# The mixing of values turned over in both attention layers: probabilities stationary, values moving, tokens on the output's partitions

## The reference, cut to what matters

```python
# x: (16, 256, 128); 16 heads of 8 channels
x = x + attn_a(layernorm(x))     # attention inside blocks of 64 positions
x = x + ffn(layernorm(x))        # 8 experts, top 2 of them per token
x = x + attn_b(layernorm(x))     # the 16 rows attend across each other at each position, with a bias,
                                 # then an output projection
x = x + ffn(layernorm(x))
# attn: softmax(q k^T * scale) @ v for each head
```

## Time and profile before

| | |
|---|---|
| median of three runs | 976.49 us |
| the profiled execution | 975.18 us |
| its span, first to last instruction | 973.4 us |
| mean granted TensorE clock | 0.878 |
| busy: TensorE matmul, weight load | 708.4 us, 583.4 us |
| busy: VectorE, ScalarE, GpSimd | 523.4, 473.5, 396.2 us |

### The profile page before, as it was taken

How to read it: one execution, slowest core, us unless ns; L and a number is a source line. 1 busy time by engine, 2 the same in 40 slices (tenths; PEclk the granted TensorE clock), 3 DMA queues, 4 the chain that set the end, 5 groups by cost and what they waited for, 6 DMA issues and landing times. The chain is left out here.

```text
span 973.4 us, 26881 instructions
## 1 busy us (share of the span) xinstructions
PE 708.4 (73%) x8764; PEld 583.4 (60%) x8765; DVE 523.4 (54%) x1810; ACT 473.5 (49%) x876; POOL 396.2 (41%) x458
## 2 busy tenths in 40 slices
PE   1688877831699999998077898761109999999940
PEld 1356555521588888887035676661108888888830
DVE  3367888863356555554253565642305555555524
ACT  0689877630355555553058897520005555555510
POOL 1223777786033333333231154588732333333320
PEclk9989999975799999999558999985559999999985
DMA  7001222212111111111330000001211111111107
GB/s 204 8 12 45 68 83 87 76 56 67 32 47 47 49 46 47 47 47 36 99 118 24 26 3 10 31 29 39 69 39 41 49 44 49 47 47 49 45 20 259
DMA packets 54045, 54.51 MB, mean 56 GB/s; under 512 B 8272, under 2 KB 43472, under 8 KB 53968
## 3 DMA queue, kind: packets, MB, share of 16 engines
q1 hardware_dynamic: 42608, 32.19, 12.1%
q0 software_dynamic: 8704, 18.11, 5.8%
q10 hardware_dynamic: 2656, 3.15, 0.9%
HBM read 29.51 MB, written 23.90 MB: 55 GB/s over the span
## 5 line engine op out<-in xcount | busy, mean ns | idle before, releaser
L1581 POOL DMA_INDIRECT expert_out<-moe_a_out,moe_a_place x72 | 69.0, 958 | 153.0 <-DVE moe_a_out L1716 153.0
L1581 POOL DMA_INDIRECT expert_out<-moe_b_out,moe_b_place x72 | 69.0, 958 | 152.7 <-DVE moe_b_out L1716 152.7
L1613 PE MATMUL wide<-wgu,moe_a_hi 128*128 x288 | 96.7, 417 | 0.5 <-issue 0.5
L1613 PE MATMUL wide<-wgu,moe_b_hi 128*128 x288 | 96.7, 417 | 0.4 <-issue 0.4
L1629 PE MATMUL wide<-wd,moe_a_hidT 128*128 x576 | 76.4, 276 | 1.1 <-DVE moe_a_out L1716 0.7
L1629 PE MATMUL wide<-wd,moe_b_hidT 128*128 x576 | 76.4, 276 | 1.0 <-DVE moe_b_out L1716 0.7
L1669 ACT ACTIVATE moe_a_glow<-wide 128x512 f32<-128x512 f32 x72 | 43.0, 598 | 69.9 <-PE wide L1613 69.8
L1669 ACT ACTIVATE moe_b_glow<-wide 128x512 f32<-128x512 f32 x72 | 43.0, 598 | 69.6 <-PE wide L1613 69.5
L441 POOL DMA_INDIRECT routed<-la_norm_x,la_place x64 | 63.6, 994 | 23.0 <-issue 19.3
L1629 PEld LDWEIGHTS wide<-wd,moe_a_hidT 128*128 128x128 f32 x576 | 70.0, 192 | 1.7 <-issue 1.7
L1629 PEld LDWEIGHTS wide<-wd,moe_b_hidT 128*128 128x128 f32 x576 | 70.0, 192 | 1.6 <-issue 1.6
(11 more groups left out here) (257 smaller groups left out, 1693.4 us busy)
## 6 DMA issues: line engine op xcount, KB each, us to landing
moe_a_rows<-routed SPq DMA_DIRECT2D x72, 66.0 KB, 1.9
moe_b_rows<-routed SPq DMA_DIRECT2D x72, 66.0 KB, 1.9
lb_outs<-expert_out SPq DMA_DIRECT2D x8, 512.0 KB
la_stage<-in_wg SPq DMA_DIRECT2D x8, 256.0 KB, 2.6
la_stage<-in_wu SPq DMA_DIRECT2D x8, 256.0 KB, 2.8
wd<-in_wd SPq DMA_DIRECT2D x8, 256.0 KB, 3.7
kept<-stream SPq DMA_DIRECT2D x8, 256.0 KB, 3.6
stream<-kept SPq DMA_DIRECT2D x8, 256.0 KB
```

The costliest lines, as they stand in the source:

```text
L1581: pool.indirect_dma_start(d.expert[:, :], bass.IndirectOffsetOnAxis(ap=place[s % 4][:, 0:1], axis=0), out[u][:, :], None).then_inc(stored[ ...
L1613: last = nc.tensor.matmul(ps[u][:, :], x[u][:, :], w(j, part), start=i == 0, stop=i == 2)
```

## The change

`mixing` swaps its operands in both layers: the transposed probabilities are loaded as weights and `stand` moves past them, so that tokens come out on the partitions and head channels on the free axis. In the first layer that is 64 stationary columns and 18 moving ones in two column strips of 64; in the second 32 stationary and 36 moving ones in four strips of 32. The number of products stays 32 in a call. `out_side`, `flip` and the memset of PSUM are gone; `divide` reads PSUM straight after `mixing`. VectorE's `divide` stands later in the first layer's iteration but belongs to the pair before (`p - 1` after `shift(p, 1)`, where it was `p - 2` after `shift(p, 0)`); in the second layer both halves of the same quad are divided in the next iteration, and `mix` there has two buffers.

```diff
@@ first_layer
-                        for b in range(2):
-                            for i in range(4):
-                                col = t * 256 + gp * P + b * BLK
+                        for i in range(4):
+                            for b in range(2):
+                                col = ((2 * t + gp) * 4 + i) * 2 * (HD + 1)
                                 last = nc.tensor.matmul(
-                                    psO[32 * i:32 * i + 2 * (HD + 1), col:col + BLK],
-                                    stand[c % 2][:, p % 2 * 2 + t, b, 4 * gp + i, :],
-                                    probT[p % 2][gp][t][:, i * P + b * BLK:i * P + (b + 1) * BLK], start=True, stop=True,
-                                    tile_position=(0, 32 * i))
+                                    psO[BLK * b:BLK * (b + 1), col:col + 2 * (HD + 1)],
+                                    probT[p % 2][gp][t][:, i * P + b * BLK:i * P + (b + 1) * BLK],
+                                    stand[c % 2][:, p % 2 * 2 + t, b, 4 * gp + i, :], start=True, stop=True,
+                                    tile_position=(0, BLK * b))
-                if behind:
-                    flip(p - 1)
...
             def divide(p):
-                dve.wait_ge(flipped, p + 1)
+                dve.wait_ge(mixed, p + 1)
...
-                if 0 <= p - 2 < PAIRS:
-                    divide(p - 2)
...
                     peak(p, 1)
                     shift(p, 1)
+                if 0 <= p - 1 < PAIRS:
+                    divide(p - 1)
...
-                if behind:
-                    out_side(p - 1)
@@ second_layer
-                        for b in range(4):
-                            for g2 in range(2):
-                                col = t2 * 256 + gp * P + b * BLK
+                        for g2 in range(2):
+                            for b in range(4):
+                                col = ((2 * t2 + gp) * 2 + g2) * 4 * (HD + 1)
                                 at = (g2 * 2 + t2) * P + b * BLK
                                 last = nc.tensor.matmul(
-                                    psO[64 * g2:64 * g2 + 4 * (HD + 1), col:col + BLK],
-                                    stand[c % 2][:, 2 * w + t2, b, 2 * gp + g2, :], probT(c, gp, w)[:, at:at + BLK],
-                                    start=True, stop=True, tile_position=(0, 64 * g2))
+                                    psO[BLK * b:BLK * (b + 1), col:col + 4 * (HD + 1)], probT(c, gp, w)[:, at:at + BLK],
+                                    stand[c % 2][:, 2 * w + t2, b, 2 * gp + g2, :], start=True, stop=True,
+                                    tile_position=(0, BLK * b))
...
-                if behind:
-                    flip(c - 1, 0)
...
-                if behind:
-                    flip(c - 1, 1)
...
                     peak(c, 0)
                     shift(c, 0)
-                if 0 <= c - 2 < QUADS:
-                    divide(c - 2, 1)
+                if 0 <= c - 1 < QUADS:
+                    divide(c - 1, 0)
...
                     shift(c, 1)
                 if 0 <= c - 1 < QUADS:
-                    divide(c - 1, 0)
+                    divide(c - 1, 1)
...
-                if behind:
-                    out_side(c - 1, 0)
...
-                if behind:
-                    out_side(c - 1, 1)
```

More of the change, by code:

```diff
@@ L338, in first_layer @@
         most = two("most", [P, HEADS])
-        side = sb("side", [P, TB])
+        steps = sb("steps", [P, STEPS])
         inv = sb("inv", [P, 2 * HEADS])
@@ L353, in first_layer @@
         r.totals, r.table_sem = totals, table_sem
-        r.row_f, r.capped = side[:, 0:STEPS], side[0:1, TB // 2:TB // 2 + STEPS + 2 * BEHIND]
+        r.row_f, r.capped = steps[:, 0:STEPS], sb("capped", [1, STEPS + 2 * BEHIND])[:, :]
         r.count_i, r.tiles_i = sb("count_i", [P, EXPERTS], I32), sb("tiles_i", [P, EXPERTS], I32)
@@ L467, in _ @@
         def _(pe):
-            pe.wait_ge(o_cleared, 1)
             def turn_x(c):
@@ L689, in divide @@
             def divide(p):
-                dve.wait_ge(flipped, p + 1)
-                out = psO.rearrange("p (i w) -> p i w", w=32)[:, :, 0:2 * (HD + 1)].rearrange("p i (g e) -> p i g e", e=HD + 1)
+                dve.wait_ge(mixed, p + 1)
+                out = psO[:, 0:16 * 2 * (HD + 1)].rearrange("p (i g e) -> p i g e", g=2, e=HD + 1)
                 inverse = inv[:, :].rearrange("p (i g) -> p i g", g=2)
@@ L843, in out_flat @@
                 nc.scalar.activation(probT[p % 2][gp][w][:, :], psP[w], ACT.Copy).then_inc(flat_copied, 1)
[L845 to L849, removed]
             def rise_gap(c):
@@ L862, in _ @@
                 even = p % 2 == 0
-                here, behind = 0 <= p < PAIRS, 0 <= p - 1 < PAIRS
+                here = 0 <= p < PAIRS
                 if here:
@@ L932, in second_layer @@
         most = two("most", [P, 2 * HEADS])
-        side = sb("side", [P, TB])
+        steps = sb("steps", [P, STEPS])
         inv = sb("inv", [P, 2 * HEADS])
-        mix = sb("mix", [P, BATCH, D])
+        mix = two("mix", [P, BATCH, D])
         mixT = sb("mixT", [P, TB])
@@ L1200, in turn_back @@
                 for t in range(BATCH):
-                    last = nc.tensor.transpose(psP[0][:, t * P:(t + 1) * P], mix[:, t, :], k.ident)
+                    last = nc.tensor.transpose(psP[0][:, t * P:(t + 1) * P], mix[c % 2][:, t, :], k.ident)
                 last.then_inc(back, 1)
@@ L1315, in divide @@
                 o = 2 * c + w
-                dve.wait_ge(flipped, o + 1)
-                out = psO.rearrange("p (i w) -> p i w", w=64)[:, :, 0:4 * (HD + 1)].rearrange("p i (g e) -> p i g e", e=HD + 1)
+                dve.wait_ge(mixed, o + 1)
+                out = psO[:, 0:8 * 4 * (HD + 1)].rearrange("p (i g e) -> p i g e", g=4, e=HD + 1)
                 inverse = inv[:, :].rearrange("p (i g) -> p i g", g=4)
@@ L1320, in divide @@
                 dve.wait_ge(inverted, o + 1)
-                if c >= 1:
-                    dve.wait_ge(back, c)
-                nc.vector.tensor_tensor(mix[:, 2 * w:2 * w + 2, :].rearrange("p t (i g e) -> p (t i) g e", g=4, e=HD),
+                if c >= 2:
+                    dve.wait_ge(back, c - 1)
+                nc.vector.tensor_tensor(mix[c % 2][:, 2 * w:2 * w + 2, :].rearrange("p t (i g e) -> p (t i) g e", g=4, e=HD),
                                         out[:, :, :, 0:HD], inverse.unsqueeze(3).to_broadcast([P, 8, 4, HD]), ALU.mult)\
@@ L1499, in _ @@
             for c in range(-3, QUADS + 6):
-                here, behind = 0 <= c < QUADS, 0 <= c - 1 < QUADS
+                here = 0 <= c < QUADS
                 if here:
                     rise_up(c, 0)
-                if behind:
-                    out_side(c - 1, 0)
                 if 0 <= c - 5 < QUADS:
```

37 lines of the change are left out of this document (8 added, 29 removed).

## The result

The changed kernel takes **997.98 us** (median of four runs, 990.08 to 1004.54); the kernel before, measured beside it, 976.7 (972.31 to 977.88). The ratio is **1.0225, with a 95% interval of 1.0153 to 1.0296**: slower by some 21 us, where 977 (968.5 to 989) was predicted. The profiled execution took 995.66 us (span 993.8, mean granted clock of TensorE 0.839; before 975.18, 973.4 and 0.878), so 20.5 us are to be found.

What follows compares the result with a forecast made beforehand. First layer bound by a ring of TensorE, VectorE and ScalarE, then GpSimd; second by TensorE and ScalarE, then GpSimd. 975.2 + 4.4 - 4.1 = 975.5, plus 1.3 to the median, gave 977 us, range 968.5 to 989.

Steps and rivals of the forecast that it cites:

- The sizes of the two mixings: A call of `mixing` takes 2.0 us in the first layer, 1.0 more, and 0.67 us in the second, 0.57 less.
- the 4.8 us of that rival: First layer's `mixing`: load and move in series over all strips, 4.8 us a call, kernel over 1015 us; chance 0.02.
- the length of the round: First layer, from one `route_logits` to the next over an odd and an even iteration: 21.4 us after the change.
- before's three long rounds: First-layer rounds of the kernel before, timed at 21.30 us, in which `project_k` waited for `spots`: +0.1 us each.
- The division's new place in the first layer: VectorE's division behind `shift(p, 1)`: VectorE comes some 0.8 us later, TensorE 0.9 later too, so it costs nothing.
- The second layer, -4.1: Second layer's net: gains of 3.1 less 0.4 for the later `measure2`, plus 1.4 of GpSimd's idle time: -4.1 us.
- 2.05 us in which VectorE stands: Second layer: VectorE's wait before each moved division, for `score` 1.29, `mixing` 0.67 and some 0.1 of signals.
- the second wait: Second layer: VectorE waiting at `divide(c - 1, 1)` behind `shift(c, 1)`, with `measure2`, `route`, `add_map` queued behind; 2.05 us.
- 0.4 for `measure2` now behind the second wait: Second layer: 0.4 us taken once off the gain of 3.1, as `measure2` comes later in VectorE's list.
- the rival with a chance of 0.13: Second layer: VectorE's waits over 2.3 us each, loop no shorter than 15.88 us, kernel 981 to 984 us; chance 0.13.
- The bound of -8 us: Second layer's largest gain: TensorE's own path 1.7 us less in each of five iterations, VectorE's waits covered.
- The dear loads: First layer's `mixing` loads in turn or at full cost, up to 3.65 us a call: kernel 999 us; chance 0.15.

Runs made afterwards that it cites:

- the kernel with 54 columns: First layer changed, second as before; each first-layer mixing matmul moves its 18 columns three times, results unchanged: 978.0 us, 1.0041 of the kernel before.
- the first layer alone: The change in the first layer only, second layer as in the kernel before: 1.0038, 1.0170 and 1.0103 of the kernel before, in three series.
- the usual conditions: Conditions of the first result and four of five experiment series, in which the kernel before takes 975 to 977 us at a granted clock of 0.87 to 0.88.
- the first series: Each half of the change by itself and variants with the divisions at their old places, measured beside the kernel before at 1025.6 us.
- the second layer alone: The change in the second layer only, first layer as in the kernel before: 1.0081, and measured again in another series 1.0062.

## Why the prediction was wrong, point by point

**The sizes of the two mixings: right, at TensorE's upper level.** 1.98 us to the next group in the first layer (2.0), 0.7 in the second (0.67; 599.06 to 599.76). Loads under other strips' matmuls, against the rule of the Trainium skill (TensorE: Matmul & The Clock Gate, The mechanism): right, as no call took the 4.8 us of that rival, even at the lower level (3.6).

**The first layer: the length of the round was right; the step that failed is that all durations were taken at TensorE's upper level.** With the clock held up by 54 or 36 columns nearly every round is 21.0 to 21.2 us (predicted 21.4), and the layer's end 0.7, 3.3 and 4.6 us later than in the profile of before (predicted 4.4). The sum fits, its parts do not quite: the prediction took the second of before's three long rounds for one of 21.3 us, and it had lasted 22.73 (133.26 to 155.99), with a stretch at the lower level in it. So over the four middle rounds the kernel with 54 columns is 0.9 us faster than before, where +1.7 was predicted, and its loss lies in front of them: `route_logits` starts at 96.45 in place of 91.94, after a mixing of 3.40 us at the lower level. The change as it is came out 9.3 us later, and 13 in the two profiles of the first layer alone. The rest is the granted clock: 0.87 to 0.93 for 0.96. It was read in the earlier trace rows and given no price; no rival had it. The runs show the cause by one knob alone, the number of columns moved, at a mixing of unchanged length: 2, 18, 36, 54 columns give 0.72, 0.87, 0.95 and 0.97 in 53 to 197 us. The first of these is of another series and holds the change's second layer as well, which does not touch this stretch. What makes the chip lower the clock behind few columns is not shown.

**The division's new place in the first layer costs nothing: right as far as the runs tell** (1.0038 with the new place, 1.0069 with the old).

**The second layer, -4.1: wrong, in two steps.** "2.05 us in which VectorE stands" holds for the second wait alone. It took for granted that TensorE starts `score(c + 1, 0)` at once on the shift; but TensorE comes there late, as `turn_x2` stands in its queue ahead, waits for GpSimd, and GpSimd for `measure2`. And the "0.4 for `measure2` now behind the second wait" was the mis-sized term: it counted the delay once, on the path to the end, where it goes round through `root2`, the normalisation and `turn_x2` in each iteration. The `root2` from which on GpSimd is full came at 653.51 us, where about 634 was predicted. The prediction had named the sign of this: wrong if VectorE's waits stand at the head of a longer loop. Moving the second division on, or back, takes the whole loss away (1.0017, 0.9993, 0.9984, against 1.0062). This was the rival with a chance of 0.13, that the waits eat the layer's gain; it had only the gain eaten, 981 to 984 us, and no loop that gets longer than before.

**The gain in the second layer** was not there without the waits either, in the usual conditions: 0.9984 and 0.9976, each interval with 1 in it. Its `root2`, from which on GpSimd is full, comes at 632.73 us in the one profile, 633.46 in the earlier trace rows. VectorE's waits before the reciprocals fell to 8.4 us, but `add_map` still waits 3.5 us for `map_out` (604.39), and the clock of 528 to 617 us was 0.91 for 1.00. Which of the two holds it back was not told apart. In the first series the same kernel gained 1.2%. The bound of -8 us was loosely set: two mixings and two flips save TensorE 2.2 us an iteration by the prediction's own terms, not 1.7, and rows give a `flip` 0.49 us there (571.06 to 571.55), not 0.55.

**The dear loads** would have given 999 us, near the measured time, by a mechanism that is not there.

**What stays open:** how the second layer's loss divides. From first `peak` to last dispatch it was +5.7 us in the second layer alone, +6.2 in one profile of the whole change and +10.0 in the other, with granted clocks of 0.90, 0.89 and 0.82 in 528 to 617 us; that the loop's waits of TensorE bring the clock down, and so make it longer, fits the timeline but was not tried by itself. Also why one and the same first layer gave 1.017, 1.010 and, in the first series, 1.004.

The best version measured is before's first layer with the second turned over and the divisions at their old places: 0.9884 in the first series, no difference that can be told in the usual conditions. No version with the first layer turned over beat the kernel before.

## What to carry to other kernels

Turning a product over so that the wide operand is loaded and the narrow one moves can leave TensorE busy and yet, as here (0.91 for 0.96 in the first layer), go with a lower granted clock in what follows: before such a change, see how the matmuls behind it last at either level, and if spare columns can be moved at no cost, try them. When a step that waits moves up in an engine's list, follow everything behind it round through the other engines until it comes back, and price it for each turn of the loop; here one place further back made the difference between a loss of 6 us and none. And take halves of a change in the same conditions as the whole before adding them up.

## What the runs showed of the hardware that was not expected

- More moving work gave less time: 978.0 us with 54 columns, 985.2 with 18 and otherwise the same kernel in the same series; with 2 columns in the changed kernel the granted clock of 53 to 90 us was 0.71 while TensorE was busy 97% of the stretch.
- The first layer's mixing (64 fp32 columns loaded, two strips) takes 2.03 to 2.08 us for 64 records, whatever it moves between 2 and 54 columns. At the lower level it takes 3.6 us in place of 2.05 (200.45 in the changed kernel).
- The same kernel took 975 to 977 us in four series and 1025.6 us in the first, 5% more. There the clock of 53 to 197 us was 0.87 and 0.86 with before's first layer (0.94 to 0.98 in the others). What made the difference is not shown.
